# Transpose copies moved from VectorE to ScalarE in the q/k/v projection stage of an attention layer (8 cores)

## The chip, the cores and the metric

One Trainium2 chip, all 8 NeuronCores, one launch. Each core computes a quarter of the tokens of one of two sequences and exchanges nothing with the others. The metric is the device time in microseconds of the slowest core, the median over runs. Engines are called TensorE (PE; PEld are its weight loads), VectorE (DVE), ScalarE (ACT), GpSimd (POOL) and SyncE (SP); POOL and SP here mostly issue DMAs.

## The reference

Input: two sequences of 8192 tokens with 1024 features, float32. One post-norm layer: attention, then a channel mix with a one-token shift.

```python
x = layernorm(x + attn(x)); x = layernorm(x + ffn(x))
# attn, 16 heads of 64
xn = (x - mean) / sqrt(var + 1e-6) * gamma + beta
q, k, v = split(xn @ Wq.T + bq), split(xn @ Wk.T + bk), split(xn @ Wv.T + bv)
s = q @ k.T / 8
s = sigmoid(s - mu) * exp(s);  s = s / s.sum(-1)
attn = merge(s @ v) @ Wo.T + bo
# ffn
xr, xk = mu_r*x + (1-mu_r)*x_prev, mu_k*x + (1-mu_k)*x_prev
ffn = sigmoid(xr @ W_r.T) * (square(relu(xk @ W_k.T)) @ W_v.T)
```

## The kernel before

The program is written instruction by instruction with hand-made semaphore counts. Every engine runs its own list in order. The counters are `pe`, `dv`, `ac` (one each for TensorE, VectorE, ScalarE) and several for DMAs; a plan made ahead of time (`pRv`, `aS2`, `aRg`, `chgv`) tells ScalarE, whose list is written first, which counts to wait for. The helper `ch` adds a count to an instruction and lets its engine wait for it.

The stages, in order of time:

1. *Weights* (L167 to L324). 56 blocks of 128x1024 floats are loaded into four buffers `wld`; VectorE scales 24 of them into the resident q, k and v weights, and casts the other 32 into `wcs` (four buffers), from where POOL stores them to `wfd` for later stages (`emit_ffn_store`, L215).
2. *Projection* (L325 to about L700). The core goes over all 8192 tokens of its sequence in 16 groups of 4 tiles of 128 tokens. For a group: SP loads four tiles `xg` (L443), each released by the normalisation of the tile four before it. ScalarE takes the sum (L652) and the sum of squares (L654) of each tile; VectorE makes mean and variance of the group (`emit_groupchain`, L669 to L672), ScalarE the inverse root by Ln and Exp (L658, L660), VectorE the last small step (L675). Then for each tile: VectorE normalises (`emit_norm`, L449), TensorE does eight 128x128 transposes into one of two PSUM tiles `tr_ps` (`emit_transpose`, L462), VectorE copies the result to `xnt_g` (`emit_trevac`, L481). `xnt_g` has room for one group. After the four tiles TensorE projects v tile by tile (L498, and L502 for the bias, two halves a tile), VectorE casts it (L520) and POOL stores it in eight pieces a tile (L531); then k for the group in eight steps (L548, L552, cast L565, store L574); in the first four groups, which are the core's own queries, q as well (L593, cast L606).
3. *Attention* (L733 to about L1000). For 5 query tiles (of width 1 and four of 512), 8 head pairs and 64 key blocks: scores (L884, L888), tanh (L815) and exp (L818) on ScalarE, their product (L932) on VectorE, weighted sum over v (L916, L920).
4. *Output projection, layer norm, channel mix* (from L1020), after each query tile and at the end.

The order in which the blocks of a group are written is the order in which each engine gets them:

```python
                for g in range(NT // 4):
                    for t in range(4 * g, 4 * g + 4):
                        emit_sync(t)
                    emit_groupchain(g)
                    for t in range(4 * g, 4 * g + 4):
                        emit_norm(t)
                        emit_transpose(t)
                        emit_trevac(t)
                    for tt2 in range(4 * g, 4 * g + 4):
                        emit_vproj(tt2)
                        emit_vevac(tt2)
                        emit_vstore(tt2)
                    emit_ktproj(g)
```

Of the kernel before, what the change touches and what calls it, by code (L numbers as in the profile page):

```python
# [41 lines left out]
def build(S, TOKQ):  # L42
# [31 lines left out]
    with ExitStack() as big:  # L74
# [86 lines left out]
        with ExitStack() as asc:  # L161
# [5 lines left out]
            with ExitStack() as psc:  # L167
                EP = psc.enter_context
                wld = [EP(nc.sbuf_tensor(f"wld{i}", [128, D], F32)) for i in range(4)]
                wcs = [EP(nc.sbuf_tensor(f"wcs{i}", [128, D], BF16)) for i in range(4)]  # L170
# [44 lines left out]
                def emit_ffn_store(g, gi):  # L215
                    g.wait_ge(dv.sem, t_dv[gi])
                    wi, c2 = gi // NB, gi % NB
                    dTs[gi % 2].inc(g.dma_start(wfd[wplan[wi]][c2], wcs[gi % 4][:]), 16)
                    assert dTs[gi % 2].v == t_st[gi]
# [69 lines left out]
                def _(v):  # L289
# [3 lines left out]
                    for wi, wn in enumerate(wplan):  # L293
                        for c2 in range(NB):
# [7 lines left out]
                            else:  # L302
                                if gi - 2 in t_st:
                                    v.wait_ge(dTs[gi % 2].sem, t_st[gi - 2])
                                if wn == "wvf":
                                    ins = v.tensor_scalar(wcs[gi % 4][:], wld[gi % 4][:],
                                                          0.5, None, AX.mult)
                                else:
                                    ins = v.tensor_copy(wcs[gi % 4][:], wld[gi % 4][:])
# [16 lines left out]
            with ExitStack() as psc:  # L326
# [108 lines left out]
                def emit_sync(t):  # L435
                    @blk.sync
                    def _(sy, t=t):
# [3 lines left out]
                        if t >= 4:  # L441
                            sy.wait_ge(dv.sem, vN[t - 4])
# [3 lines left out]
                def emit_norm(t):  # L446
                    @blk.vector
                    def _(v, t=t):
# [4 lines left out]
                        vN[t] = dv.v  # L453

                def emit_transpose(t):
                    @blk.tensor
                    def _(tn, t=t):
                        tn.wait_ge(dv.sem, vN[t])
                        if (t % 2) in last_tr_evac:
                            tn.wait_ge(dv.sem, last_tr_evac[t % 2])  # L460
# [8 lines left out]
                def emit_trevac(t):  # L469
                    @blk.vector  # L470
                    def _(v, t=t):
                        v.wait_ge(pe.sem, pR[t])
                        if t >= 4:
                            t4 = t - 4
                            v.wait_ge(pe.sem, pV[t4])
                            hh4 = t4 // 4
                            if (hh4, NB - 1) in pK:
                                v.wait_ge(pe.sem, pK[hh4, NB - 1])
                            if (hh4, NB - 1) in pQ:
                                v.wait_ge(pe.sem, pQ[hh4, NB - 1])  # L480
                        ins = v.tensor_copy(  # L481
                            xnt_g[:, :, 128 * (t % 4):128 * (t % 4 + 1)],
                            tr_ps[t % 2][:].rearrange("p (b w) -> p b w", b=NB))
                        dv.inc(ins)
                        vE[t] = dv.v
                        last_tr_evac[t % 2] = dv.v
                        v.wait_ge(dv.sem, dv.v)

                def emit_vproj(t):
                    @blk.tensor  # L490
                    def _(tn, t=t):
                        tn.wait_ge(dv.sem, vE[t])
# [44 lines left out]
                def emit_ktproj(hh):  # L537
                    for d2 in range(NB):
# [4 lines left out]
                        def _(tn, hh=hh, d2=d2, bk=bk):  # L543
                            tn.wait_ge(dv.sem, vE[4 * hh + 3])
# [35 lines left out]
                def emit_qproj(hh):  # L580
                    lq = 512 * hh + 1
                    qw = min(512, TOKQ - 512 * hh)
                    for d2 in range(NB):
# [4 lines left out]
                        def _(tn, hh=hh, d2=d2, qw=qw, bk=bk):  # L588
                            tn.wait_ge(dv.sem, vE[4 * hh + 3])
# [27 lines left out]
                dXv, aS2, aRg, chgv, pRv = {}, {}, {}, {}, {}  # L617
                cvx, cpx = dvB2, peB2
                for g in range(NG4):
                    chgv[g] = cvx + 4  # L620
                    cvx += 5
                    for t in range(4 * g, 4 * g + 4):
                        cvx += 2
                        cpx += 1
                        pRv[t] = cpx
                    cvx += 8
                    cpx += 8
                    hh = g
                    cvx += 8
                    cpx += 8  # L630
                    if hh in QHALVES:
                        cvx += 8
                        cpx += 8
                cax = acB
                for g in range(NG4):
# [5 lines left out]
                    aRg[g] = cax  # L641

                @blk.scalar
                def _(s):
                    for g in range(NG4):
# [16 lines left out]
                        assert ac.v == aRg[g]  # L662

# [14 lines left out]
                for g in range(NT // 4):  # L678
# [3 lines left out]
                    for t in range(4 * g, 4 * g + 4):  # L682
                        emit_norm(t)
                        emit_transpose(t)
                        emit_trevac(t)
# [8 lines left out]
                a_end_dv, a_end_pe = dv.v, pe.v  # L694
# [6 lines left out]
        with ExitStack() as bscope:  # L701
# [83 lines left out]
            with ExitStack() as prosc:  # L785
                xtp = [prosc.enter_context(nc.psum_tensor(f"xtp{i}", [128, 512], F32))
                       for i in range(4)]
                emit_xt_prep(0, a_end_dv, xtp,
                             sync_gate=[(pe.sem, a_end_pe), (dv.sem, a_end_dv)])
# [762 lines left out]
```

## Time and profile before

| | |
|---|---|
| median of 3 runs | 6676.42 us (6671.8 to 6680.95) |
| the profiled execution's own time | 6689.89 us |
| its span (first to last instruction of the slowest core, core 7) | 6688.4 us |
| spans of the other cores | 6646.9 us (core 1) to 6688.1 us (core 6) |
| busy over the span | PE 70%, ACT 69%, DVE 53%, PEld 19%, POOL 12% |
| chain that ended last | ACT 47%, PE 17%, DVE 14%, issue 13%, DMA 5%, POOL 3% |

The profile is one execution, read on core 7 if nothing else is said. About 1.5 us of the execution lie outside the span. Times of the timeline count from the span's start. A row of a group gives the busy time, the mean duration of one instruction, and the time for which its engine stood idle just before such instructions, with what released it. The columns of a stretch are the busy time of PE, PEld, DVE, ACT and POOL, then the granted clock of TensorE (1.00 is 2.4 GHz, 0.50 is 1.2 GHz), the share of DMA time, and GB/s.

### The profile page before, as it was taken

To read this page: it belongs to the slowest core of one execution; us is meant where nothing else is said; L and a number is where in the kernel's file an instruction comes from. 1 tells how busy PE (TensorE), PEld (TensorE's weight loads), DVE (VectorE), ACT (ScalarE), POOL (GpSimd) and SP (SyncE) were. 2 spreads that over 40 slices of the span, in tenths; PEclk is the share of its full clock that TensorE was granted. 3 is DMA by queue.
4 is the path that set the end of the run, shared out by engine and by line. 5 is a ranking of instruction groups with operands and counts; after the bars stand their busy time and mean duration, and the time that the engine had idled before them with its cause. 6 is when DMAs were issued, how large, how long until landed. Compare 5 with 4: busy or idle time off the path is not lost.

```text
span 6688.4 us, 68687 instructions; the slowest of 8 cores (6646.9 to 6688.4 us)
## 1 busy us (share of the span) xinstructions
PE 4700.1 (70%) x15252; PEld 1254.7 (19%) x15252; DVE 3569.5 (53%) x3930; ACT 4600.4 (69%) x5573; POOL 821.0 (12%) x1540
## 2 busy tenths in 40 slices
PE   3677777767777776777777677777767777775544
PEld 0233333531111111111111111111111111111212
DVE  2233333346666665666666566666656666665342
ACT  0211112769999995999999599999959999993111
POOL 2224433210000000000000000000000000000111
PEclk7788887555555556555555655555565555556767
DMA  7222222431111111111111111111111111111221
GB/s 219 71 64 80 79 79 82 119 91 32 32 31 31 32 33 41 32 32 32 30 33 32 42 32 33 32 30 32 32 42 32 32 32 31 31 32 33 63 63 63
DMA packets 182633, 332.78 MB, mean 50 GB/s; under 512 B 37354, under 2 KB 119274, under 8 KB 182260
## 3 DMA queue, kind: packets, MB, share of 16 engines
q0 software_dynamic: 73664, 185.17, 8.8%
q1 hardware_dynamic: 108596, 143.22, 7.7%
q8 instruction: 163, 2.67, 0.2%
q14 instruction: 210, 1.72, 0.1%
HBM read 277.39 MB, written 50.86 MB: 49 GB/s over the span
## 4 chain that ended last, share of the span: by engine, by line
ACT 47%; PE 17%; DVE 14%; issue 13%; DMA 5%; POOL 3%; DVEq 1%; ACTq 0%; SPq 0%; POOLq 0%
ACT tbf L815 35%; ACT ebf L818 11%; DVE wbf L932 5%; PE pr_ps L1242 3%; POOL vd L531 3%; PE o_ps L916 2%; PE st_ps L884 2%; PE pjp L498 2%; DMA ktd<-ktev 2%; DVE dinvb L949 1%; PE pp L1042 1%; PE o_ps L920 1%; PE trp L462 1%; PE ktp L593 1%; PE o_ps L896 1%
## 5 line engine op out<-in xcount | busy, mean ns | idle before, releaser
L932 DVE SCALAR_TENSOR_TENSOR wbf<-tbf,ebf 128x1024 bf16<-128x1024 bf16 (+1 forms) x2560 | 2592.7, 1014 | 1812.1 <-ACT ebf L818 1746.3
L815 ACT ACTIVATE tbf<-st_ps,mubc 128x1024 bf16<-128x1024 f32 (+1 forms) x2560 | 2954.0, 1154 | 349.8 <-PE st_ps L888 216.4
L818 ACT ACTIVATE ebf<-st_ps,ln2b 128x1024 bf16<-128x1024 f32 (+1 forms) x2560 | 2962.2, 1157 | 0.0
L916 PE MATMUL o_ps<-wbf,vbx 128*65 128x512 bf16 (+1 forms) x2560 | 1323.9, 517 | 1149.7 <-DVE wbf L932 1120.6
L920 PE MATMUL o_ps<-wbf,vbx 128*65 128x512 bf16 (+1 forms) x2560 | 1374.2, 537 | 0.0
L884 PE MATMUL st_ps<-qt_sb,ktb 64*128 64x512 bf16 (+1 forms) x2560 | 1297.2, 509 | 84.3 <-ACT ebf L818 75.2
L888 PE MATMUL st_ps<-qt_sb,ktb 64*128 64x512 bf16 (+1 forms) x2560 | 1312.4, 515 | 0.0
L848 POOL DMA_DIRECT2D ktb<-ktd x640 | 343.1, 536 | 4360.0 <-PE st_ps L888 4283.7
L916 PEld LDWEIGHTS o_ps<-wbf,vbx 128*65 128x65 bf16 x2560 | 334.3, 131 | 2218.3 <-issue 2188.7
L884 PEld LDWEIGHTS st_ps<-qt_sb,ktb 64*128 64x128 bf16 x2560 | 253.8, 100 | 1701.4 <-issue 1676.7
L658 ACT ACTIVATE stv<-stv,epsA 128x4 f32<-128x4 f32 x16 | 4.8, 297 | 591.7 <-DVE stv L672 591.7
L920 PEld LDWEIGHTS o_ps<-wbf,vbx 128*65 128x65 bf16 x2560 | 395.6, 155 | 0.0
L531 POOL DMA_DIRECT2D vd<-vev x512 | 271.3, 538 | 444.7 <-DVE vev L520 441.1
L498 PE MATMUL pjp<-wv_sb,xnt_g 128*128 128x512 bf16 x1024 | 268.4, 409 | 0.0
L548 PE MATMUL ktp<-xnt_g,wk_sb 128*128 128x512 bf16 x1024 | 245.4, 383 | 21.4 <-DVE ktev L565 21.3
L888 PEld LDWEIGHTS st_ps<-qt_sb,ktb 64*128 64x128 bf16 x2560 | 256.1, 101 | 0.0
L1379 ACT ACT_TABLE_LOAD x4 | 5.1, 1283 | 318.9 <-PE pr_ps L1321 318.9
L520 DVE CAST vev<-pjp 128x512 bf16<-128x512 f32 x128 | 88.6, 692 | 234.2 <-PE pjp L502 138.5
L462 PE MATMUL trp<-idb,xntk 128*128 128x128 bf16 x512 | 64.4, 305 | 190.5 <-DVE xntk L449 190.5
L565 DVE CAST ktev<-ktp 128x512 bf16<-128x512 f32 x128 | 88.6, 692 | 196.6 <-DMA ktd<-ktev 157.8
L1111 ACT ACT_TABLE_LOAD x5 | 6.4, 1283 | 266.8 <-DVE rowB L1101 266.8
L1242 PE MATMUL pr_ps<-ka_sb,wch 128*128 128x512 bf16 x256 | 71.8, 450 | 114.2 <-DVE ka_sb L1287 87.3
(191 smaller groups left out, 2500.4 us busy)
## 6 DMA issues: line engine op xcount, KB each, us to landing
vbx<-vd SPq DMA_DIRECT2D x640, 132.0 KB, 2.1
ktb<-ktd POOLq DMA_DIRECT2D x640, 128.0 KB, 2.4
xg<-xkv SPq DMA_DIRECT2D x64, 512.0 KB, 3.8
vd<-vev POOLq DMA_DIRECT2D x512, 33.0 KB, 3.3
ktd<-ktev POOLq DMA_DIRECT2D x128, 128.0 KB, 2.1
woh_sb<-wos POOLq DMA_DIRECT2D x80, 128.0 KB, 2.7
xq<-xkv SPq DMA_DIRECT2D x16, 512.0 KB, 6.1
wch<-wrs POOLq DMA_DIRECT2D x32, 256.0 KB, 3.3
```

Source lines behind the costliest of these rows:

```text
L498: tn.matmul(pj_ps[bk][:], xnt_g[:, c2, 128 * (t % 4):128 * (t % 4 + 1)], wv_sb[:, c2, 512 * hf:512 * (hf + 1)], start=(c2 == 0), stop=False)
L531: ins = g.dma_start(vd[p2, t // 4, :, 132 * (t % 4):132 * (t % 4) + 132], v_ev[t % 2][:, p2, :])
L548: tn.matmul(kt_ps[bk][:], wk_sb[:, c2, 128 * d2:128 * (d2 + 1)], xnt_g[:, c2, 0:512], start=(c2 == 0), stop=False)
L815: ac.inc(s.activation(tbuf[k % WBUF][:].rearrange("p (h w) -> p h w", h=2)[:, :, 0:W], srcv, AF.Tanh, bias=mubc[:], scale=0.5))
L818: a2.inc(s.activation(ebuf[k % WBUF][:].rearrange("p (h w) -> p h w", h=2)[:, :, 0:W], srcv, AF.Exp, bias=ln2b[:], scale=1.0))
L848: ins = g.dma_start(ktb[c2 % 4][:], ktd.rearrange("(p r) s -> p r s", r=128)[p2][:, 512 * c2:512 * (c2 + 1)])
L884: tn.matmul(st_ps[:, sgl:sgl + W], ktb[c2 % 4][0:64, 128 * j:128 * (j + 1)], qt_sb[0:64, p2, qo:qo + W], start=True, stop=True, tile_posit ...
L888: mm = tn.matmul(st_ps[:, sgl + 512:sgl + 512 + W], ktb[c2 % 4][64:128, 128 * j:128 * (j + 1)], qt_sb[64:128, p2, qo:qo + W], start=True, ...
L916: tn.matmul(o_ps[par][0][0:65, 0:W], vb[c2 % 4][:, 132 * j:132 * j + 65], wbuf[k2 % WBUF][:, 0:W], start=(k2 == 0), stop=(k2 == KS - 1))
L920: mm = tn.matmul(o_ps[par][1][0:65, 0:W], vb[c2 % 4][:, 132 * j + 66:132 * j + 131], wbuf[k2 % WBUF][:, 512:512 + W], start=(k2 == 0), sto ...
L932: s1.inc(v.scalar_tensor_tensor(vw(wbuf[k % WBUF][:]), vw(tbuf[k % WBUF][:]), 1.0, vw(ebuf[k % WBUF][:]), op0=AX.add, op1=AX.mult))
L1242: mm = tn.matmul(pr_ps[:, 4 * h + j, 0:W], wch[c][:, 128 * (4 * wb + j):128 * (4 * wb + j + 1)], rhs[:, c, 0:W], start=(c == 0), stop=(c = ...
```

## The change

In the projection stage the copy of the transposed tile from `tr_ps` to `xnt_g` leaves VectorE's list (`emit_trevac` is gone) and becomes an Identity activation in ScalarE's list, four in a row after the Ln and Exp of the group. The transposes wait for the copy of the tile two before them, and the projections for the copies, by ScalarE's counter instead of VectorE's. The counts are planned ahead for more instructions (`vNv`, `pVv`, `pKv`, `pQv`, `vEa`), and SP's wait uses a planned count. SP's first load of the attention stage waits for ScalarE's counter too. Apart from that, the buffers `wcs` of the weight stage are two instead of four.

```diff
--- before.py
+++ after.py
@@ -167,7 +167,7 @@
...
-                wcs = [EP(nc.sbuf_tensor(f"wcs{i}", [128, D], BF16)) for i in range(4)]
+                wcs = [EP(nc.sbuf_tensor(f"wcs{i}", [128, D], BF16)) for i in range(2)]
@@ -215,7 +215,7 @@
...
-                    dTs[gi % 2].inc(g.dma_start(wfd[wplan[wi]][c2], wcs[gi % 4][:]), 16)
+                    dTs[gi % 2].inc(g.dma_start(wfd[wplan[wi]][c2], wcs[gi % 2][:]), 16)
@@ -303,10 +303,10 @@
                                 if gi - 2 in t_st:
                                     v.wait_ge(dTs[gi % 2].sem, t_st[gi - 2])
                                 if wn == "wvf":
-                                    ins = v.tensor_scalar(wcs[gi % 4][:], wld[gi % 4][:],
+                                    ins = v.tensor_scalar(wcs[gi % 2][:], wld[gi % 4][:],
                                                           0.5, None, AX.mult)
                                 else:
-                                    ins = v.tensor_copy(wcs[gi % 4][:], wld[gi % 4][:])
+                                    ins = v.tensor_copy(wcs[gi % 2][:], wld[gi % 4][:])
@@ -439,7 +439,7 @@
...
                         if t >= 4:
-                            sy.wait_ge(dv.sem, vN[t - 4])
+                            sy.wait_ge(dv.sem, vNv[t - 4])
                         dXs[t % 4].inc(sy.dma_start(xg[t % 4][:], xr[t]), 16)
@@ -451,13 +451,14 @@
...
                         vN[t] = dv.v
+                        assert dv.v == vNv[t]
 
                 def emit_transpose(t):
                     @blk.tensor
                     def _(tn, t=t):
                         tn.wait_ge(dv.sem, vN[t])
-                        if (t % 2) in last_tr_evac:
-                            tn.wait_ge(dv.sem, last_tr_evac[t % 2])
+                        if t >= 2:
+                            tn.wait_ge(ac.sem, vEa[t - 2])
                         for b2 in range(NB):
                             mm = tn.transpose(tr_ps[t % 2][:, 128 * b2:128 * (b2 + 1)],
                                               xn_tok[t % 4][:, 128 * b2:128 * (b2 + 1)],
@@ -466,30 +467,10 @@
...
-                def emit_trevac(t):
-                    @blk.vector
-                    def _(v, t=t):
-                        v.wait_ge(pe.sem, pR[t])
-                        if t >= 4:
-                            t4 = t - 4
-                            v.wait_ge(pe.sem, pV[t4])
-                            hh4 = t4 // 4
-                            if (hh4, NB - 1) in pK:
-                                v.wait_ge(pe.sem, pK[hh4, NB - 1])
-                            if (hh4, NB - 1) in pQ:
-                                v.wait_ge(pe.sem, pQ[hh4, NB - 1])
-                        ins = v.tensor_copy(
-                            xnt_g[:, :, 128 * (t % 4):128 * (t % 4 + 1)],
-                            tr_ps[t % 2][:].rearrange("p (b w) -> p b w", b=NB))
-                        dv.inc(ins)
-                        vE[t] = dv.v
-                        last_tr_evac[t % 2] = dv.v
-                        v.wait_ge(dv.sem, dv.v)
-
                 def emit_vproj(t):
                     @blk.tensor
                     def _(tn, t=t):
-                        tn.wait_ge(dv.sem, vE[t])
+                        tn.wait_ge(ac.sem, vEa[t])
@@ -541,7 +522,7 @@
...
-                            tn.wait_ge(dv.sem, vE[4 * hh + 3])
+                            tn.wait_ge(ac.sem, vEa[4 * hh + 3])
@@ -586,7 +567,7 @@
...
-                            tn.wait_ge(dv.sem, vE[4 * hh + 3])
+                            tn.wait_ge(ac.sem, vEa[4 * hh + 3])
@@ -614,23 +595,31 @@
...
                     for t in range(4 * g, 4 * g + 4):
-                        cvx += 2
+                        cvx += 1
+                        vNv[t] = cvx
...
+                    for t in range(4 * g, 4 * g + 4):
+                        cpx += 2
+                        pVv[t] = cpx
+                        cvx += 2
@@ -639,6 +628,9 @@
                         aS2[t] = cax
                     cax += 2
                     aRg[g] = cax
+                    for t in range(4 * g, 4 * g + 4):
+                        cax += 1
+                        vEa[t] = cax
@@ -660,6 +652,21 @@
                         ch(s, ac, s.activation(stv[:, 4 * g:4 * g + 4], stv[:, 4 * g:4 * g + 4],
                                                AF.Exp, scale=-0.5))
                         assert ac.v == aRg[g]
+                        for t in range(4 * g, 4 * g + 4):
+                            s.wait_ge(pe.sem, pRv[t])
+                            if t >= 4:
+                                t4 = t - 4
+                                s.wait_ge(pe.sem, pVv[t4])
+                                hh4 = t4 // 4
+                                if (hh4, NB - 1) in pKv:
+                                    s.wait_ge(pe.sem, pKv[(hh4, NB - 1)])
+                                if (hh4, NB - 1) in pQv:
+                                    s.wait_ge(pe.sem, pQv[(hh4, NB - 1)])
+                            ch(s, ac, s.activation(
+                                xnt_g[:, :, 128 * (t % 4):128 * (t % 4 + 1)],
+                                tr_ps[t % 2][:].rearrange("p (b w) -> p b w", b=NB),
+                                AF.Identity))
+                            assert ac.v == vEa[t]
@@ -682,7 +689,6 @@
                     for t in range(4 * g, 4 * g + 4):
                         emit_norm(t)
                         emit_transpose(t)
-                        emit_trevac(t)
                     for tt2 in range(4 * g, 4 * g + 4):
                         emit_vproj(tt2)
                         emit_vevac(tt2)
@@ -691,7 +697,7 @@
...
-                a_end_dv, a_end_pe = dv.v, pe.v
+                a_end_dv, a_end_pe, a_end_ac = dv.v, pe.v, ac.v
@@ -786,7 +792,8 @@
...
-                             sync_gate=[(pe.sem, a_end_pe), (dv.sem, a_end_dv)])
+                             sync_gate=[(pe.sem, a_end_pe), (dv.sem, a_end_dv),
+                                        (ac.sem, a_end_ac)])
```

## Rows read from the trace of the kernel before

**Rows 1.** The page's costly groups; columns: busy us, mean ns, idle us before, releaser

```profile
L815 ACT ACTIVATE tbf<-st_ps,mubc 128x1024 bf16<-128x1024 f32 (+1 forms) x2560 | 2954.0, 1154 | 349.8 <-PE st_ps L888 216.4
```

**Rows 2.** Busy us of each engine in 100 us stretches, granted clock, DMA

```profile
600.00:700.00 100.00, 78.83 (x341) 31.07 (x340) 33.64 (x55) 16.11 (x31) 42.52 (x80) 0.86 0.24 79
...
1500.00:1600.00 100.00, 75.41 (x187) 13.84 (x186) 63.45 (x50) 93.68 (x94) 5.90 (x11) 0.50 0.11 31
```

**Rows 3.** Groups by shape, 190 to 1110 us, core 7

```profile
L531 POOL DMA_DIRECT2D vd<-vev x512 | 271.3, 538 | 444.7 <-DVE vev L520 441.1 <-issue 1.9
...
L498 PE MATMUL pjp<-wv_sb,xnt_g 128*128 128x512 bf16 x1024 | 268.4, 409 | 0.0
...
L548 PE MATMUL ktp<-xnt_g,wk_sb 128*128 128x512 bf16 x1016 | 243.5, 383 | 21.4 <-DVE ktev L565 21.3
...
L520 DVE CAST vev<-pjp 128x512 bf16<-128x512 f32 x128 | 88.6, 692 | 234.2 <-PE pjp L502 138.5 <-DMA vd<-vev 91.6 <-DVE vev L520 3.8
...
L565 DVE CAST ktev<-ktp 128x512 bf16<-128x512 f32 x126 | 87.2, 692 | 194.6 <-DMA ktd<-ktev 155.8 <-PE ktp L552 32.4 <-DVE ktev L565 4.3
...
L652 ACT ACTIVATE xntk<-xg 128x1024 bf16<-128x1024 f32 x64 | 67.6, 1056 | 115.7 <-DMA xg<-xkv 104.1 <-PE trp L462 8.7 <-PE pjp L502 2.2
...
L462 PE MATMUL trp<-idb,xntk 128*128 128x128 bf16 x512 | 64.4, 305 | 190.5 <-DVE xntk L449 190.5
...
L481 DVE COPY xnt_g<-trp 128x1024 bf16<-128x1024 bf16 x64 | 44.3, 692 | 98.7 <-PE trp L462 98.7
...
L658 ACT ACTIVATE stv<-stv,epsA 128x4 f32<-128x4 f32 x16 | 4.8, 297 | 591.7 <-DVE stv L672 591.7
...
L652 ACT ACT_TABLE_LOAD x1 | 1.3, 1283 | 9.7 <-DMA xg<-xkv 9.7
```

**Rows 4.** Timeline of one group head; columns: start us, duration us

```profile
685.84 1.90 PE L548 MATMUL ktp<-xnt_g,wk_sb 128*128 128x512 bf16 x8
...
687.67 0.38 PE L552 MATMUL ktp<-ones_r,bke 1*128 1x512 bf16 x1
...
692.01 0.81 DVE L449 TENSOR_SCALAR xntk<-xg,stv,stn 128x1024 bf16<-128x1024 f32 x1
...
693.08 1.01 PE L462 MATMUL trp<-idb,xntk 128*128 128x128 bf16 x8 [5.02 <-DVE xntk L449]
...
694.33 0.69 DVE L481 COPY xnt_g<-trp 128x1024 bf16<-128x1024 bf16 x1 [1.51 <-PE trp L462]
...
695.13 0.81 DVE L449 TENSOR_SCALAR xntk<-xg,stv,stn 128x1024 bf16<-128x1024 f32 x1
...
696.19 1.01 PE L462 MATMUL trp<-idb,xntk 128*128 128x128 bf16 x8 [2.11 <-DVE xntk L449]
...
702.43 1.01 PE L462 MATMUL trp<-idb,xntk 128*128 128x128 bf16 x8 [2.11 <-DVE xntk L449]
...
703.24 2.34 PE L498 MATMUL pjp<-wv_sb,xnt_g 128*128 128x512 bf16 x5
```

**Rows 5.** Groups from 0 to 250 us, the weight casts

```profile
L309 DVE CAST wcs<-wld 128x1024 bf16<-128x1024 f32 x24 | 16.8, 698 | 54.4 <-DMA wos<-wcs 21.0 <-DMA wrs<-wcs 19.2 <-DMA wkfs<-wcs 13.8
```

**Rows 6.** ScalarE's groups by shape, whole span

```profile
L815 ACT ACTIVATE tbf<-st_ps,mubc 128x1024 bf16<-128x1024 f32 x2048 | 2816.3, 1375 | 273.3 <-PE st_ps L888 172.8 <-DVE wbf L932 100.4
...
L1379 ACT ACTIVATE osb<-pr_ps 128x1024 f32<-128x1024 f32 x16 | 16.4, 1024 | 41.8 <-DMA out<-osb 41.0 <-ACT dump_c L1383 0.6
```

**Rows 7.** Stretches of 1 us around that head; PEclk follows POOL

```profile
692.00:693.00 1.00, 0.00 (x0) 0.00 (x0) 0.81 (x1) 0.00 (x0) 0.00 (x0) 0.71 0.00 0
...
706.00:707.00 1.00, 1.00 (x5) 0.20 (x3) 0.00 (x0) 0.88 (x1) 0.00 (x0) 0.96 0.00 0
```

**Rows 8.** Timeline of TensorE at the next group's head

```profile
755.62 1.91 PE L498 MATMUL pjp<-wv_sb,xnt_g 128*128 128x512 bf16 x4
```

**Rows 9.** A stretch of 1 us in that next group

```profile
760.00:761.00 1.00, 1.00 (x4) 0.39 (x3) 0.64 (x1) 0.94 (x1) 0.00 (x0) 0.65 0.00 0
```

**Rows 10.** Waits on core 0, 200 to 1110 us: us in total, times, longest

```profile
DVE ktev L565 <- DMA ktd<-ktev: 116.8, 64, 5.0
```

More of the change, by code:

```diff
@@ L616, in build @@
                 NG4 = NT // 4
-                dXv, aS2, aRg, chgv, pRv = {}, {}, {}, {}, {}
+                dXv, aS2, aRg, chgv, pRv, vNv = {}, {}, {}, {}, {}, {}
                 cvx, cpx = dvB2, peB2
+                pVv, pKv, pQv, vEa = {}, {}, {}, {}
                 for g in range(NG4):
@@ L622, in build @@
                     for t in range(4 * g, 4 * g + 4):
-                        cvx += 2
+                        cvx += 1
+                        vNv[t] = cvx
                         cpx += 1
                         pRv[t] = cpx
-                    cvx += 8
-                    cpx += 8
+                    for t in range(4 * g, 4 * g + 4):
+                        cpx += 2
+                        pVv[t] = cpx
+                        cvx += 2
                     hh = g
-                    cvx += 8
-                    cpx += 8
+                    for d2 in range(NB):
+                        cpx += 1
+                        pKv[(hh, d2)] = cpx
+                        cvx += 1
                     if hh in QHALVES:
-                        cvx += 8
-                        cpx += 8
+                        for d2 in range(NB):
+                            cpx += 1
+                            pQv[(hh, d2)] = cpx
+                            cvx += 1
                 cax = acB
```

## Prediction

> **What bounds the kernel now.** I read the page's costly groups first. The bulk of the span is attention: ScalarE's two activations per key block, of which L815 alone is busy 2954 us [rows 1], alternate with VectorE's product, and the change leaves that code alone. So the next view is the table of stretches: at 600 to 700 us TensorE is the busiest engine (78.8 of 100 us, granted clock 0.86) and ScalarE has 16 us of work, while at 1500 to 1600 us ScalarE has 93.7 us [rows 2]. The first of these is the projection stage, from about 200 to 1110 us, and the change lies there.
>
> In that stage's groups [rows 3] the reader should look for what TensorE waits on. It stands 190.5 us before the 64 sets of transposes, always for VectorE's normalisation (L449), and only 21.4 us before the k projections (for the k cast). ScalarE has 37 us of idle time a group (591.7 / 16) before L658. VectorE waits 98.7 us for the transposes. The timeline of one group head shows why [rows 4]: TensorE has its last k matmul at 688.05; then come the small statistics chain and the first normalisation, and the first transposes start at 693.08. From there four tiles go through one serial loop: transposes, 1.25 us later VectorE's copy (0.69), 0.11 later the next normalisation (0.81), 0.25 later the next transposes: 1.25 + 0.69 + 0.11 + 0.81 + 0.25 = 3.11 us a tile. VectorE is in order, and the next tile's normalisation is queued behind this tile's copy. The v projection starts 0.81 us after the fourth transposes began: 3 x 3.11 + 0.81 = 10.15, against 703.24 - 693.08 = 10.16 measured. The other groups take 9.66 to 10.88. A check on the count: 48 waits of 2.11 us are 101 of the 190.5 us; the first wait of each group makes up the rest.
>
> **The change part by part.** *Weight casts in two buffers instead of four:* cast gi already waits for the store of gi - 2, and this wait is what the trace shows before L309 [rows 5]. With two buffers the same wait protects the reuse. Nothing is later: 0.
>
> *Four normalisations in a row on VectorE:* they no longer stand behind a copy, so they end 0.81 us apart, and tiles 1 to 3 are ready before TensorE can take them.
>
> *The copy on ScalarE:* 64 Identity activations of 128x1024 from PSUM to bf16, which the trace does not have. Nearest rows: the same function from PSUM to float, 1.024 us; from SBUF to bf16, 1.056 us (L652); tanh from two PSUM banks in the busiest stage, 1.375 us on average; VectorE's own copy of this very tile, 0.69 us [rows 3, 6]. I take 1.04, by the two Identity rows, and keep 0.69 and 1.38 as ends. The table of functions needs no exchange: 16 Ln and 16 Exp run between the Identity and Square activations now, and the stage shows one load of a table (1.28 us), at its first tile [rows 3].
>
> *The new chain, from the first transposes (0):* the second set can start at 0.83. The first copy runs from 1.25 to 2.29, the second from about 2.39 to 3.43. There are two PSUM tiles, so the third set waits for the first copy (2.29 + 0.25 = 2.54) and the fourth for the second (3.43 + 0.25 = 3.68). The v projection starts at 3.68 + 0.81 = 4.49, or 2.41 + 2E for a copy of E. The third and fourth copies are beside the projection, whose first tile needs only the first copy. Saved: 10.16 - 4.49 = 5.67 us a group, x 16 = 90.7 us. With E = 1.38 it is 80; with E = 0.69 it is 101 (the transposes and copy still follow each other as above).
>
> *What is queued behind the copies on ScalarE:* the statistics of the next group, 8 x (1.056 + 0.186) = 9.9 us. The 4 copies add 4.2 us and the group is 5.7 us shorter, so the 37 us of slack fall to about 27: hidden. What VectorE no longer does (0.69 x 64 = 44 us) lay in the loop already counted; nothing more comes of it.
>
> *SP:* the four loads of xg for the next group are still released by the normalisations, now 0.8 instead of 3.1 us apart, so 2 MB are asked for almost at once. Their readers come 27 us early: 0. POOL issues 40 stores a group, 40 x 0.54 = 21.6 of some 57 us (910 / 16): it does not set the pace, and its stores start from the v casts, so they move with the projection.
>
> *The clock.* Full speed is 1.00 of granted clock (2.4 GHz), 0.50 is 1.2 GHz. TensorE's last work before this head ended at 688.05; the clock fell in the microsecond from 692, before the first transposes, and rose at 706, 2.8 us after the projection began [rows 7]. The stand before the transposes does not change, so the fall stays. The rise came 1.8 to 5.1 us after the start of the projection in the sixteen groups (5.1 in the one whose projection began at 755.62 [rows 8, 9]), 3.5 on average. At half clock half of that time is lost: 16 x 3.5 / 2 = 28 us is the most that an earlier rise could give. After the change the transposes fill some 3.4 of the last 4.5 us before the projection instead of 3.4 of 10.2, but with pauses of 0.7 us still in them. I keep 0 and 28 as ends and take 6, near the row that exists.
>
> *Sum:* 90.7 + 6 = 97 us. Against the profiled execution's own time, 6689.9 - 97 = 6593; that execution lies 13.5 us above the median of the three runs, so 6676.4 - 97 = 6579 is the forecast for the median.
>
> **The rivals.**
> (B) *The clock comes back before the projection.* The four sets of transposes are counted as steady work and almost no matmul of the projection runs at half clock. For it: the transposes stand closer. Against it: the pauses left between them. 90.7 + 28 = 119 us: 6557.
>
> (C) *Part of the gain goes to the stores.* The next group's loads come in one burst, and the v stores follow about 5.7 us sooner. On core 7 VectorE waits 155.8 us for landings of k stores and 91.6 us for v stores, on core 0 116.8 us for k stores [rows 3, 10], so landings differ by core and the slower cores, which end last, have least room. Against it: TensorE itself stood only 21.4 us for all this, 1.3 us a group. If that became three times as much, 2.8 us more a group, 45 us are lost: 6676 - 97 + 45 = 6624.
>
> (D) *The chain stays serial with a longer copy.* If the next normalisation or transposes still waited for the copy, each of three loops a group grows by 1.04 - 0.69 = 0.35 us and by a hand-over of 0.25 instead of 0.11: 16 x 3 x 0.49 = 24 us more, 6700. It decides where the copies no longer overlap the other tiles, or where one copy takes over (10.16 - 2.41) / 2 = 3.9 us. Against it: the code issues four normalisations with no wait on ScalarE between them, and the longest comparable activation is 1.38 us. The Trainium skill (ScalarE: Activation LUTs, Rules for kernel authors) speaks for this side: simple elementwise work belongs on VectorE, which it calls up to about three times faster in bf16. By that rule alone the move costs time. The trace agrees on the single copy (0.69 against 1.02 to 1.06), but the copy's length is not what the loop is made of.
>
> (E) *No change:* the stage is paced by something that the head hides, as the stores. The idle time before the transposes then comes back before the k projections. 6676. Against it: up to the end of the group TensorE takes its k matmuls without a pause, eight in 1.90 us [rows 4].
>
> **How the numbers follow.** Chances: forecast 0.68, B 0.12, C 0.14, D 0.03, E 0.03. The forecast's own ends: 80 us without a clock term (6596) and 101 + 6 (6569). B with the shortest copy would be 6547. The range 6551 to 6618 holds the forecast, B and the nearer half of C. A measurement of this kernel tells 0.2% (13 us) from no change. Faster by more than that: forecast, B and C, 0.94; within: E, 0.03; slower: D, 0.03.
>
> **What would show it.** In the changed profile: L449 four times in a row, 0.8 us apart; the copy on ScalarE 1.0 to 1.1 us long, 64 times; first transposes to first v matmul 4.5 us instead of 10.2; TensorE's idle time before the transposes near 190 - 91 = 100 us; the stretch from 200 us to the first attention work some 95 us shorter, and attention as long as now. The prediction is wrong if the copy takes 2 us or more, if the wait before L548 grows by more than 2 us a group, or if attention itself changes.

## The result, and the profile after

| | before | after |
|---|---|---|
| median (range, runs) | 6678.68 us (6671.8 to 6752.65, 10) | 6588.61 us (6574.29 to 6665.75, 10) |
| profiled execution | 6689.89 us | 6581.74 us |
| span of its slowest core | 6688.4 us (core 7) | 6580.2 us (core 5) |
| ratio | | 0.9871, 95% interval 0.984 to 0.9902 |

The change makes the kernel 1.3% faster. 6579 was predicted, with a range of 6551 to 6618. In a few executions, here and in the experiments, the cores of one die ran at a lower clock and took longer; the medians hold them, the ratios leave them out.

I cut every profile in two: the projection stage from the first transposes to the first scores, and the rest up to the end of the span, each as the mean of the eight cores. The stage took 896.4 us before (887.9 to 912.0) and 801.1 us after (791.4 to 805.5): 95.3 us less. The rest took 5563.8 and 5561.5 us. In all kernels below the rest stays between 5560 and 5571 us, so the stage is what they are compared by. Two profiles of one kernel still differ in it by 4.5 us (the changed kernel) and 8.4 us (e2).

The stage in parts, as means of the eight cores. A head runs from a group's first transposes to its first v matmul; a2 is the changed kernel profiled a second time:

| us | before | after | a2 |
|---|---|---|---|
| the 16 heads | 165.7 | 72.3 | 71.7 |
| TensorE idle before the first transposes of the 15 later groups | 66.2 | 68.4 | 68.7 |
| all else (v, k and q projections) | 664.4 | 660.4 | 656.2 |
| of it: TensorE idle before the k and q projections | 9.0 | 13.9 | 11.2 |
| of it: at half clock, from the start of the v projection to the rise | 58.1 | 37.9 | 35.5 |
| stage | 896.4 | 801.1 | 796.6 |

The groups by shape of the stage after the change (190 to 1030 us, core 5), which answer to [rows 3]:

```profile
L529 PE MATMUL ktp<-xnt_g,wk_sb 128*128 128x512 bf16 x1024 | 243.1, 380 | 11.5 <-DVE ktev L546 11.5
...
L546 DVE CAST ktev<-ktp 128x512 bf16<-128x512 f32 x128 | 88.5, 692 | 173.9 <-DMA ktd<-ktev 141.4 <-PE ktp L533 25.5 <-DVE ktev L546 4.6
L501 DVE CAST vev<-pjp 128x512 bf16<-128x512 f32 x128 | 88.5, 692 | 296.3 <-PE pjp L483 181.2 <-DMA vd<-vev 111.0 <-DVE vev L501 3.8
...
L665 ACT ACTIVATE xnt_g<-trp 128x1024 bf16<-128x1024 bf16 x64 | 65.6, 1025 | 54.7 <-PE trp L463 41.5 <-ACT xnt_g L665 12.8
L463 PE MATMUL trp<-idb,xntk 128*128 128x128 bf16 x512 | 61.4, 302 | 101.2 <-DVE xntk L449 88.6 <-ACT xnt_g L665 12.2 <-issue 0.2
...
L650 ACT ACTIVATE stv<-stv,epsA 128x4 f32<-128x4 f32 x16 | 4.8, 299 | 473.6 <-DVE stv L679 473.6
L644 ACT ACT_TABLE_LOAD x1 | 1.3, 1283 | 10.5 <-DMA xg<-xkv 10.5
```

TensorE's idle time before the transposes (now L463) fell from 190.5 to 101.2 us. What is left before the normalisation, 88.6 us, is one wait of a group (5.5 us); the 12.2 us for ScalarE are the two short waits for a PSUM tile. The idle time before the k projections (now L529) is 11.5 us against 21.4, but these are two different cores, each the slowest of its run: on the mean of the eight it grew, from 9.0 to 13.9 us with the q projections. The copy on ScalarE takes 1025 ns, 64 times. ScalarE's slack before the Ln is 473.6 / 16 = 29.6 us a group, where it was 37. There is still one load of a table.

The timeline of a group head after the change (core 5), which answers to [rows 4]:

```profile
680.19 0.69 DVE L546 CAST ktev<-ktp 128x512 bf16<-128x512 f32 x1 [1.11 <-DMA ktd<-ktev]
...
683.11 2.98 DVE L449 TENSOR_SCALAR xntk<-xg,stv,stn 128x1024 bf16<-128x1024 f32 x4
...
684.18 1.86 PE L463 MATMUL trp<-idb,xntk 128*128 128x128 bf16 x16 [5.06 <-DVE xntk L449]
685.40 1.02 ACT L665 ACTIVATE xnt_g<-trp 128x1024 bf16<-128x1024 bf16 x1 [2.66 <-PE trp L463]
...
686.56 1.01 PE L463 MATMUL trp<-idb,xntk 128*128 128x128 bf16 x8 [0.52 <-ACT xnt_g L665]
686.68 1.03 ACT L665 ACTIVATE xnt_g<-trp 128x1024 bf16<-128x1024 bf16 x1 [0.26 <-ACT xnt_g L665]
...
687.85 1.01 PE L463 MATMUL trp<-idb,xntk 128*128 128x128 bf16 x8 [0.27 <-ACT xnt_g L665]
...
688.65 2.41 PE L479 MATMUL pjp<-wv_sb,xnt_g 128*128 128x512 bf16 x8
```

Four normalisations stand in one row of 2.98 us. From the first transposes to the first v matmul there are 688.65 - 684.18 = 4.47 us, where there were 10.16. The other groups have 4.18 to 4.75. In front of the head nothing is better: 5.06 us of idle TensorE, as before (5.02).

Stretches of the same core: 100 us of the stage, 100 us of attention, and two microseconds of the head above:

```profile
600.00:700.00 100.00, 87.85 (x393) 35.66 (x392) 32.53 (x54) 35.40 (x59) 47.53 (x90) 0.93 0.26 90
1500.00:1600.00 100.00, 78.32 (x200) 14.65 (x200) 60.68 (x51) 100.00 (x101) 6.43 (x12) 0.50 0.12 34
682.00:683.00 1.00, 0.00 (x0) 0.00 (x0) 0.21 (x2) 0.51 (x2) 0.00 (x0) 0.93 0.32 131
689.00:690.00 1.00, 1.00 (x4) 0.40 (x3) 0.00 (x0) 0.76 (x1) 0.00 (x0) 0.65 1.03 418
```

TensorE's busy time in this stretch of the stage went from 78.8 to 87.9 of 100 us [rows 2]. The clock still falls in each head (here late in the microsecond from 682, while TensorE stands), and it rises in the microsecond from 689, about one microsecond after the projection began; before, it came back 2.8 us after [rows 7].

### The profile page after: what moved, and what is told of

Its sections match the earlier page's. It is cut to its first block, busy times and chain, and to the rows that moved or that the text cites. A ratio compares the mean times of both kernels' runs of the same rounds, so it can differ in the third digit from the quotient of the medians.

```text
span 6580.2 us, 68688 instructions; the slowest of 8 cores (6557.6 to 6580.2 us)
## 1 busy us (share of the span) xinstructions
PE 4714.6 (72%) x15252; PEld 1256.0 (19%) x15252; DVE 3520.5 (54%) x3866; ACT 4672.0 (71%) x5637; POOL 821.7 (12%) x1540
## 4 chain that ended last, share of the span: by engine, by line
ACT 49%; PE 18%; DVE 13%; issue 12%; DMA 4%; POOL 2%; ACTq 1%; DVEq 0%; POOLq 0%; SPq 0%
ACT tbf L822 36%; ACT ebf L825 11%; DVE wbf L939 5%; PE pr_ps L1249 3%; PE o_ps L923 2%; PE pjp L479 2%; PE st_ps L891 2%; POOL vd L512 2%; DVE dinvb L956 1%; DMA ktd<-ktev 1%; PE o_ps L927 1%; PE ktp L529 1%; PE pp L1049 1%; PE ktp L574 1%; PE o_ps L903 1%
## 5 line engine op out<-in xcount | busy, mean ns | idle before, releaser
L650 ACT ACTIVATE stv<-stv,epsA 128x4 f32<-128x4 f32 x16 | 4.8, 299 | 473.6 <-DVE stv L679 473.6
L529 PE MATMUL ktp<-xnt_g,wk_sb 128*128 128x512 bf16 x1024 | 243.1, 380 | 11.5 <-DVE ktev L546 11.5
L546 DVE CAST ktev<-ktp 128x512 bf16<-128x512 f32 x128 | 88.5, 692 | 173.9 <-DMA ktd<-ktev 141.4
L463 PE MATMUL trp<-idb,xntk 128*128 128x128 bf16 x512 | 61.4, 302 | 101.2 <-DVE xntk L449 88.6
```

The costliest lines, as they stand in the source:

```text
L529: tn.matmul(kt_ps[bk][:], wk_sb[:, c2, 128 * d2:128 * (d2 + 1)], xnt_g[:, c2, 0:512], start=(c2 == 0), stop=False)
```

## The experiments

Each is compared with the kernel before on the same chip. "Stage" is the length defined above; two rows of one edit are two runs of it.

| | median us (range, runs) | before there | ratio, 95% interval | stage us |
|---|---|---|---|---|
| e1_wcs_only | 6705.22 (6686.9 to 6759.44, 10) | 6688.91 | 1.0026 (1.0 to 1.0053) | 895.6 |
| e2_order_only | 6600.01 (6584.58 to 6614.38, 4) | 6688.91 | 0.9861 (0.9817 to 0.9906) | 799.8 |
| e2b_order_only | 6588.81 (6581.18 to 6639.83, 4) | 6685.65 | 0.9876 (0.9837 to 0.9914) | 791.4 |
| e3_serial_act | 6705.16 (6690.79 to 6782.44, 11) | 6688.91 | 1.0018 (0.9993 to 1.0043) | 910.4 |
| e4_copy_twice | 6628.06 (6617.19 to 6641.15, 5) | 6688.91 | 0.9899 (0.9862 to 0.9936) | 837.3 |
| a2_after | 6583.85 (6580.55 to 6692.84, 5) | 6685.65 | 0.9857 (0.9839 to 0.9875) | 796.6 |
| f1_norms_early | 6513.14 (6507.6 to 6522.04, 4) | 6685.65 | 0.9751 (0.9734 to 0.9767) | 730.9 |
| f1b_norms_early | 6520.99 (6506.25 to 6548.32, 4) | 6682.14 | 0.9762 (0.9733 to 0.9792) | 740.3 |
| f5_norms_early_dve | 6571.43 (6549.77 to 6624.15, 4) | 6685.65 | 0.9845 (0.98 to 0.989) | 774.9 |
| e6_after_4kt | 6558.18 (6557.08 to 6558.53, 4) | 6682.14 | 0.9813 (0.9796 to 0.9829) | 780.0 |
| f6_early_4kt | 6467.33 (6464.28 to 6554.19, 4) | 6682.14 | 0.9676 (0.966 to 0.9692) | 688.7 |

### The weight buffers alone

The kernel before, with `wcs` in two buffers:

```diff
-                wcs = [EP(nc.sbuf_tensor(f"wcs{i}", [128, D], BF16)) for i in range(4)]
+                wcs = [EP(nc.sbuf_tensor(f"wcs{i}", [128, D], BF16)) for i in range(2)]
```

> The kernel before with the weight-cast buffers wcs two instead of four, nothing else. Theory: each cast waits already for the store two before it, so the time is that of the kernel before within 10 us (6679), and the first transposes start at the same time (201 to 211 us over the cores). Rival: two buffers make casts or stores late, the first transposes start later by 5 us or more.

Its groups from 0 to 250 us on its slowest core:

```profile
L309 DVE CAST wcs<-wld 128x1024 bf16<-128x1024 f32 x24 | 16.9, 702 | 53.8 <-DMA wos<-wcs 20.2 <-DMA wrs<-wcs 18.7 <-DMA wkfs<-wcs 14.6
```

The waits are those of [rows 5] (53.8 us against 54.4). The first transposes start at 205.5 us and before at 205.6 (means of the cores), and the stage takes 895.6 against 896.4 us. Its median lies 0.26% above, with an interval that touches 1.0; no part of its profile accounts for that. The buffers give nothing.

### The order alone, and the engine alone

In e2 the kernel before gets the order of the change, and the copies stay on VectorE:

```diff
                     for t in range(4 * g, 4 * g + 4):
                         emit_norm(t)
+                    for t in range(4 * g, 4 * g + 4):
                         emit_transpose(t)
                         emit_trevac(t)
```

> The kernel before with one thing changed: the four normalisations of a group stand ahead of its four copies in VectorE's list; the copies stay on VectorE (0.69 us). Theory (the gain came from taking the copies out of the way of the next normalisation, not from the engine): normalisations end at 2.2 us after the first transposes, the two first copies at 2.99 and 3.79, the v projection starts at 4.9 us instead of 10.2, 5.3 x 16 = 85 us, with some clock gain 6678.7 - 90 = about 6589, within 10 us of the changed kernel. Rival (VectorE had to be relieved): its 64 copies of 0.69 us stay in the chain, so 44 us or more of the gain are missing, 6633 or slower.

In e3 the changed kernel gets the old order back; the copies are on ScalarE, and each normalisation waits for the copy of the tile before:

```diff
                 def emit_norm(t):
                     @blk.vector
                     def _(v, t=t):
+                        if t % 4:
+                            v.wait_ge(ac.sem, vEa[t - 1])
```

> The changed kernel with one wait more: within a group, the normalisation of a tile waits on VectorE for ScalarE's copy of the tile before. The copies stay on ScalarE, the chain is serial again. Theory: a tile takes 1.25 + 1.02 + 0.25 + 0.81 + 0.25 = 3.58 us, the v projection starts 11.6 us after the first transposes, 1.4 x 16 = 22 us slower than the kernel before: 6701. Rival (the engine was what counted, VectorE free of 44 us of copies): faster than the kernel before, 6635 or less.

A head of e2 (timeline, core 0):

```profile
638.23 2.98 DVE L449 TENSOR_SCALAR xntk<-xg,stv,stn 128x1024 bf16<-128x1024 f32 x4
...
639.30 1.86 PE L462 MATMUL trp<-idb,xntk 128*128 128x128 bf16 x16 [5.23 <-DVE xntk L449]
641.13 0.68 DVE L481 COPY xnt_g<-trp 128x1024 bf16<-128x1024 bf16 x1
...
641.95 2.01 PE L462 MATMUL trp<-idb,xntk 128*128 128x128 bf16 x16 [0.79 <-DVE xnt_g L481]
642.12 0.69 DVE L481 COPY xnt_g<-trp 128x1024 bf16<-128x1024 bf16 x1 [0.31 <-DVE xnt_g L481]
...
644.19 2.63 PE L498 MATMUL pjp<-wv_sb,xnt_g 128*128 128x512 bf16 x7 [0.22 <-DVE xnt_g L481]
```

The first copy must wait for the end of the fourth normalisation (641.13), but then the copies are short. The head is 644.19 - 639.30 = 4.89 us. That is core 0's; core 6 has the same, and the other six cores have 4.46 us in the median, as much as after the change (4.47). The means of all 128 heads are 4.65 and 4.51 us. The stage is 799.8 and 791.4 us in the two runs (e2 and e2b), and 801.1 and 796.6 in the two of the full change. So the one added line of e2 brings the whole gain, and the change of engine adds nothing that can be measured (by the mean heads it would be 16 x 0.14 = 2 us, less than two runs of one kernel differ by).

> The kernel before with only the order of VectorE's list changed (four normalisations, then four copies, all on VectorE), again, beside the changed kernel on the same chip. If the order is the whole effect: within 10 us of the changed kernel, the stage within 5 us of 801. If ScalarE adds something of its own: slower than the changed kernel by more than 10 us.

The same place in e3 (timeline, core 0):

```profile
642.10 0.79 PE L465 MATMUL trp<-idb,xntk 128*128 128x128 bf16 x8 [4.21 <-DVE xntk L451]
643.09 1.02 ACT L667 ACTIVATE xnt_g<-trp 128x1024 bf16<-128x1024 bf16 x1 [2.44 <-PE trp L465]
644.22 0.81 DVE L451 TENSOR_SCALAR xntk<-xg,stv,stn 128x1024 bf16<-128x1024 f32 x1 [2.38 <-ACT xnt_g L667]
...
645.29 1.01 PE L465 MATMUL trp<-idb,xntk 128*128 128x128 bf16 x8 [2.40 <-DVE xntk L451]
...
653.35 3.00 PE L481 MATMUL pjp<-wv_sb,xnt_g 128*128 128x512 bf16 x7 [0.22 <-issue]
```

It is the serial loop of before with a longer copy: 3.41 us a tile (3.11 before), a head of 11.25 us in this group and 11.05 in the median of all 128 (10.31 before), and a stage of 910.4 us, 14 more than before, where 22 were expected; the heads alone are 11.5 of the 14. This is rival D, made real: moving the copy without the new order costs time (ratio 1.0018; its interval reaches to both sides of 1, and the stage says which way).

### A copy of double length

Each copy of the changed kernel is done twice (the work is repeated, nothing is left out):

```diff
-                            ch(s, ac, s.activation(
+                            for rp in range(2):
+                                ch(s, ac, s.activation(
...
-                        cax += 1
+                        cax += 2
                         vEa[t] = cax
```

> The changed kernel with each copy done twice on ScalarE, one after the other, before it is reported. Theory (the head is 2.41 us and two copies long): a copy and its repeat take about 2.3 us, the v projection starts at 7.0 us instead of 4.47, 2.55 x 16 = 41 us slower than the changed kernel, 6630; all four extra copies together would be 4 x 1.28 x 16 = 82 us, and are not all paid. Rival (the copies are hidden): as the changed kernel, 6589.

```profile
614.90 1.87 PE L463 MATMUL trp<-idb,xntk 128*128 128x128 bf16 x16 [5.32 <-DVE xntk L449]
616.12 2.14 ACT L666 ACTIVATE xnt_g<-trp 128x1024 bf16<-128x1024 bf16 x2 [2.66 <-PE trp L463]
...
618.40 1.01 PE L463 MATMUL trp<-idb,xntk 128*128 128x128 bf16 x8 [1.64 <-ACT xnt_g L666]
...
620.80 1.01 PE L463 MATMUL trp<-idb,xntk 128*128 128x128 bf16 x8 [1.39 <-ACT xnt_g L666]
...
622.03 2.94 PE L479 MATMUL pjp<-wv_sb,xnt_g 128*128 128x512 bf16 x7 [0.22 <-ACT xnt_g L666]
```

That is core 0's timeline. The head is 7.13 us. The chain of the prediction puts the fourth transposes at 1.6 + 2 x 2.14 = 5.88 us, and they start at 620.80 - 614.90 = 5.90. The projection follows them after 1.23 us, where 0.81 was taken. This 0.42 us is no matter of e4: in every trace here, the kernel before's too, two of the eight cores take longer over this step than the other six (see the last section), and I did not find what it is. Over all 128 heads the mean is 6.75 us against 4.51 in the changed kernel, and 2.24 x 16 are 36. The stage is 36 and 41 us longer than in its two runs. So two copies, the first two, stand in the head, and the other two do not.

### What the change left: the statistics chain and the first normalisation

After the change TensorE still stands 5 us in front of each head. In f1 the statistics chain and the normalisations of the next group are put into VectorE's list among this group's k casts (after the third, and after the fourth to seventh), so that the transposes find their tiles ready:

```diff
+                        if hh + 1 < NG4 and d2 == 2:
+                            emit_groupchain(hh + 1)
+                        if hh + 1 < NG4 and 3 <= d2 <= 6:
+                            emit_norm(4 * hh + 1 + d2)
...
+                for t in range(4):
+                    emit_sync(t)
+                emit_groupchain(0)
+                for t in range(4):
+                    emit_norm(t)
...
                     for t in range(4 * g, 4 * g + 4):
-                        emit_norm(t)
                         emit_transpose(t)
```

> The changed kernel with the statistics chain and the four normalisations of the next group moved ahead in VectorE's list, in between the k casts of this group. Theory (what is left of the head is the 4 to 5 us from the last projection to the first transposes, in which the clock falls, and it is a matter of order as well): the transposes follow the last projection at once, the clock stays at 1.00, the head from the last projection to the next is about 3.6 us instead of 9.2, and the first v matmuls run at full speed: (5.6 + 1.2) x 15 = 102 us less, the stage about 699 us, the whole about 102 us faster than the changed kernel. Rival (the stores set the pace once the head is gone): VectorE's waits for landings grow and TensorE stands before the k or v projections instead, less than 50 us are gained.

> f1 again, unaltered, as the measure for f6 on the same chip: the stage about 731 us.

On the same chip as f1 the changed kernel itself ran once more (a2):

> The changed kernel again, unaltered, as the measure for the three runs beside it on the same chip. Stage from the first transposes to the first scores about 801 us on average over the cores.

f1's timeline on core 0, a head and, further down, the k projections of the same group:

```profile
646.22 0.38 PE L533 MATMUL ktp<-ones_r,bke 1*128 1x512 bf16 x1
646.53 1.07 PE L463 MATMUL trp<-idb,xntk 128*128 128x128 bf16 x16
...
650.25 1.89 PE L479 MATMUL pjp<-wv_sb,xnt_g 128*128 128x512 bf16 x8
...
679.07 0.69 DVE L546 CAST ktev<-ktp 128x512 bf16<-128x512 f32 x1 [6.39 <-DMA ktd<-ktev]
...
679.90 1.89 PE L529 MATMUL ktp<-xnt_g,wk_sb 128*128 128x512 bf16 x8 [1.64 <-DVE ktev L546]
```

The transposes follow the last projection at once, the head is 3.72 us (4.22 in the mean of all 128), and in 11 of the 15 later heads of this core the granted clock stays at 1.00. The stage is 730.9 us, 66 to 70 less than after the change; 102 were expected. In f1b it is 740.3, but cores 4 and 5 took 764 and 766 us there, at a granted clock of 0.81 for some 320 us of the stage; the mean of its other six cores is 732.2. The last two lines show where the rest is: a k cast stood 6.39 us for the landing of a store, and TensorE behind it. On the mean of the cores TensorE stands 22.7 us before the k and q projections (13.9 after the change). The theory then: the landings that were hidden in the pause of the head are now on the path. It is tested further down.

f5 is f1 with the copies back on VectorE, to see whether the engine matters there:

```diff
-                            tn.wait_ge(ac.sem, vEa[t - 2])
+                            tn.wait_ge(dv.sem, vE[t - 2])
...
                         emit_transpose(t)
+                        emit_trevac(t)
```

> As f1, but with the copies on VectorE. Theory: with the normalisations out of the head, the head is two copies long on either engine, and VectorE's are shorter (0.69 against 1.02 us), but queue behind the last k or q cast: about 0.3 us a group less or equal, within 10 us of f1. Rival (VectorE has too much to do there): slower than f1 by more than 10 us.

Timeline, core 0:

```profile
565.01 1.07 PE L463 MATMUL trp<-idb,xntk 128*128 128x128 bf16 x16
...
567.90 0.69 DVE L566 CAST ktev<-ktp 128x512 bf16<-128x512 f32 x1 [2.93 <-DMA ktd<-ktev]
...
568.70 0.81 DVE L449 TENSOR_SCALAR xntk<-xg,stv,stn 128x1024 bf16<-128x1024 f32 x1
...
569.43 0.68 DVE L566 CAST ktev<-ktp 128x512 bf16<-128x512 f32 x1
...
570.42 0.69 DVE L482 COPY xnt_g<-trp 128x1024 bf16<-128x1024 bf16 x1 [0.31 <-DVE ktev L566]
...
571.26 2.01 PE L463 MATMUL trp<-idb,xntk 128*128 128x128 bf16 x16 [5.18 <-DVE xnt_g L482]
...
573.06 3.62 PE L499 MATMUL pjp<-wv_sb,xnt_g 128*128 128x512 bf16 x8
```

In f1 the first copy starts 0.83 us after the first transposes; here that would be 565.84. The copy stands in VectorE's list behind a cast that waits for a landing, the last normalisation and the last cast, and starts at 570.42; the head is 8.05 us, and the clock falls. The stage is 774.9 us, 44 more than f1 on the same chip, where less than 10 was expected: the rival holds. Here the copy on ScalarE is worth that, and in e2 it was worth nothing.

### More room for the k stores

The theory on f1's shortfall is tested by four buffers `kt_ev` instead of two, each with a semaphore of its own: e6 is the changed kernel with them, f6 is f1 with them.

```diff
-                kt_ev = [EP(nc.sbuf_tensor(f"ktev{i}", [128, 512], BF16)) for i in range(2)]
+                kt_ev = [EP(nc.sbuf_tensor(f"ktev{i}", [128, 512], BF16)) for i in range(4)]
+                kst = dKs + dWs
...
-                            if (hh, d2 - 2) in gK:
-                                v.wait_ge(dKs[d2 % 2].sem, gK[hh, d2 - 2])
+                            if (hh, d2 - 4) in gK:
+                                v.wait_ge(kst[d2 % 4].sem, gK[hh, d2 - 4])
```

> The changed kernel with four buffers for the k casts (ktev) instead of two, each with a semaphore of its own. It asks how much of the gain the stores take. Theory: in the changed kernel TensorE stands only about 12 us before the k projections, and the last k cast of a group, which waits for the landing of a store, makes the start of the next group 0.6 us late on average: 12 + 16 x 0.6 = 22 us at most, the stage about 780 us instead of 797 to 801. Rival (the stores hold back much more than TensorE's idle time shows): 45 us or more.

> f1 (normalisations of the next group between the k casts) with four buffers for the k casts. In f1 the periods of the groups without q are about 41 us, against 34.4 for the matmuls and 3.7 for the head. Theory (the missing 3 us a group are k casts that wait for landings of stores, which the two buffers and the v stores queued before them cause): most of 16 x 3 = 48 us comes back, the stage about 690 us, 40 us faster than f1. Rival (POOL's issue or the transfers themselves set the pace): the wait moves to the v casts, less than 15 us faster than f1.

The groups by shape of e6 (190 to 985 us, core 4):

```profile
L530 PE MATMUL ktp<-xnt_g,wk_sb 128*128 128x512 bf16 x1024 | 243.3, 380 | 0.0
...
L547 DVE CAST ktev<-ktp 128x512 bf16<-128x512 f32 x128 | 88.5, 692 | 145.4 <-PE ktp L534 121.6 <-DMA ktd<-ktev 18.4 <-DVE vev L502 3.1
```

The wait for landings goes from 141.4 (core 5 of the changed kernel) to 18.4 us and TensorE never waits for a k cast on this core. The stage is 780.0 us, 17 to 21 less than after the change: small, since most of those waits were beside TensorE's work. On the mean of the cores TensorE's idle time fell by 13.5 us before the k and q projections and by 6.0 before the later groups' first transposes. The groups of f6 (190 to 930 us, core 0) and 100 us of its stage:

```profile
L547 DVE CAST ktev<-ktp 128x512 bf16<-128x512 f32 x128 | 88.4, 691 | 90.7 <-PE ktp L534 86.2 <-DVE stn L695 3.5 <-DVE vev L502 0.5
```

```profile
600.00:700.00 100.00, 94.49 (x461) 38.09 (x468) 40.74 (x69) 33.33 (x52) 51.84 (x98) 1.00 0.36 121
```

The k casts wait for no landing at all. The granted clock of this core is 1.00 from the second group on, and 10 of its 11 periods of groups without q are 38.1 to 38.2 us (one 38.39). The stage is 688.7 us, 42 less than f1, and equal within 1.3 us on the eight cores. TensorE stands 0.4 us before the k and q projections, where it stood 22.7 in f1: it sets the pace. This is the fastest version here: 6467.33 us, 0.9676 of before.

## Why the prediction was right

- **The serial loop is what the head was made of: shown.** The sum 3.68 + 0.81 = 4.49 us came out as 4.47. Some of that closeness is luck: the step from a copy to the transposes behind it took 0.14 us where 0.25 was taken, and the one from the first copy to the second 0.26 where 0.10 was taken, so the third transposes start 2.38 us after the first (2.54 worked out) and the fourth 3.67 (3.68). The gain of the heads is (10.16 - 4.47) x 16 = 91 us by the two heads shown and 93.4 by all of them, where 90.7 was forecast. e3 puts the loop back and loses all of it; e2 removes only the order that made it and keeps all of it.
- **The copy:** 1.025 us, taken as 1.04 from the two Identity rows [rows 3, 6].
- **The weight buffers:** 0, shown by e1.
- **The statistics behind the copies:** slack of 29.6 us a group, worked out as 27.
- **The clock:** the fall stays, as said. On the mean of the eight cores the clock rose 3.6 us after the start of the projection before and 2.4 us after (3.5 before on core 7, as the prediction has it). Its way of counting makes 20.2 / 2 = 10 us of the half-speed time that went, where 6 was taken. Rival B, 28 us, did not happen. That the pauses between the transposes kept the rest is argued, not shown; e4 fits, with pauses of 1.6 and 1.4 us and a rise 3.7 us after the start. (The transposes fill 3.8 us of a head before by [rows 4], not the 3.4 of the prediction.)
- **The sum:** 97 us predicted, 95.3 us less in the stage, and this nearness is in part luck. The heads gave 93.4 and the clock 10.1, together 6.8 more than forecast. Against it stand two terms that the prediction put at nothing: TensorE's idle time before the k and q projections grew by 4.9 us, and that before the later groups' first transposes by 2.2. 93.4 + 10.1 - 4.9 - 2.2 = 96.4, so about 1 us is left. VectorE's waits for landings grew as well (means of the cores, k stores 138 to 147 us, v stores 88 to 96). In a2 the same two terms are 2.2 and 2.5 us, so their size differs from run to run. The medians of this comparison differ by 90 us and those of a2's by 102.
- **Rival C** (part goes to the stores, 45 us) did not happen at its size: 4.9 us of it did. What the k stores cost at all in the changed kernel is e6's 17 to 21 us. Its mechanism came late: f1 fell short of the 102 us expected by about a third, and f6, with room for the stores, gave 42 us back.
- **Rival D** needed the old order; e3 shows it, 14 us of stage (24 were worked out). The Trainium skill's rule that simple elementwise work belongs on VectorE (ScalarE: Activation LUTs, Rules for kernel authors; its row names relu, max, min, add and mul, not a copy) agrees with the single copy, 0.69 against 1.025 us. It does not decide about the kernel: with the new order both engines give the same stage, and with the early normalisations the slower copy is 44 us better.

What the prediction left out: its chain has the new order and the new engine together, and it did not ask what each is worth. With four copies of 0.69 us behind the four normalisations the chain gives a head of 4.9 us, as e2's expectation has it, and that could have been worked out from [rows 4] as well; it measured 4.46 us on six cores and 4.89 on two.

## What to carry to other kernels

Before moving work to another engine, write the same work in another order on its own engine: an in-order list that alternates "make" and "copy out" for each tile pays the whole loop for each tile, and two loops instead of one gave all of the 95 us for a line. Then look at what stands in the list behind a wait for a landing: that, and not the length of the instruction, decided here where the copy belonged. And a pause that is removed uncovers the next wait, so give its buffers room at the same time: early normalisations brought 66 to 70 us alone and two more k buffers 17 to 21, and both together 108 to 112.

## What the runs showed of the hardware

- On core 0 the granted clock fell in no head of f6 after the first, and TensorE's pauses in such a head are 0.93 and 0.67 us long; it fell at each later head of the kernel after, on cores 0 and 5 alike, during the idle stretch or less than 1 us behind it (5.06 us long in the head shown), and in the head of f5 shown during one of 5.18 us.
- In each of the 13 traces two of the eight cores take longer than the others from the start of the fourth transposes to the first v matmul: 1.23 against 0.81 us at half clock, 0.66 against 0.44 at full clock (f1, f1b, f6). They are cores 2 and 4 in before, after, a2, e2b, f1 and f5, and cores 0 and 6 in the others. The cause is open.
- In f1 cores 6 and 7 ran at a granted clock of 0.81 for 157 us of the stage (eight k matmuls in 2.28 us instead of 1.90), and took 724 and 732 us, no more than the other six (730 to 734): their idle time before the k and q projections was 7.1 and 5.4 us instead of 22 to 34.
- Four loads of 512 KB asked for within 2.5 us of each other landed 5.6 us after their issue in the median of the kernel after, and the stretch from 689 us shows them at 418 GB/s. Before, the loads were released 3.1 us apart and landed in 3.8 us. Yet ScalarE's 104.1 us of waits for them [rows 3] are gone: its fourth copy ends at 690.26, about when they have landed.
- The Identity activation of 128x1024 from PSUM took 1025 ns into bf16 and 1024 into float [rows 6].
